# A mixture-of-experts layer: residual rows added by GpSimd's stores between expert tiles, and a last stage of one copy

## What is computed

```python
xn = _layernorm(x, axis=-1)
x = x + _L1_attn_ref(xn, ...) + _L1_ffn_ref(xn, ...)
return x

# _L1_attn_ref ends with        return resid + out
# _L1_ffn_ref, for each token, over its two chosen experts:
act = silu(gh) * xh                       # h = x @ w1[e] + b1[e], split in two
out_e = act @ w2[e] + b2[e]
return jnp.sum(sel * weights[..., None], axis=2)
```

## Time and profile before

| | us |
|---|---|
| median of 3 runs | 2629.0 (2627.3 to 2629.4) |
| the profiled execution | 2626.0 |
| its span, first to last instruction | 2624.3 |
| layer0, routing and mamba, up to | 1879 |
| experts | 1879.0 to 2586.7 |
| combine | 2586.7 to 2624.3 |

### The profile page before, as it was taken

The page is one execution under the profiler, slowest core; times in us unless marked ns, Lnnn a source line. Parts: engine busy times, 40 slices in busy tenths (PEclk is TensorE's granted clock), DMA queues, the critical chain, the costliest instruction groups (busy, mean ns, idle before and its releaser), DMA issues. The chain is left out here.

```text
span 2624.3 us, 34884 instructions
## 1 busy us (share of the span) xinstructions
PE 2141.1 (82%) x10642; PEld 1531.1 (58%) x10642; DVE 1947.4 (74%) x2684; ACT 1373.9 (52%) x2317; POOL 1343.0 (51%) x953
## 2 busy tenths in 40 slices
PE   2799999999936777878787878776499999999992
PEld 1578777778721222324232324233299999999992
DVE  6654456554540898989898989899588888888882
ACT  1332223323216766666666666653277767767760
POOL 1102222112204989898989898987213433333331
PEclk8899999999966999999999999999899999999996
DMA  8011011110021222222222222222356666666646
GB/s 258 16 41 40 0 40 40 40 40 20 20 72 40 81 78 88 85 91 78 101 76 96 83 96 76 93 84 83 127 213 233 220 214 216 227 229 228 216 151 204
DMA packets 117624, 290.90 MB, mean 111 GB/s; under 512 B 21076, under 2 KB 94180, under 8 KB 98740
## 3 DMA queue, kind: packets, MB, share of 16 engines
q1 hardware_dynamic: 103252, 271.38, 29.5%
q0 software_dynamic: 14304, 18.75, 3.5%
HBM read 239.24 MB, written 50.85 MB: 111 GB/s over the span
## 5 line engine op out<-in xcount | busy, mean ns | idle before, releaser
L1004 POOL TENSOR_TENSOR m_work<-m_ux,m_bb 128x1024 f32<-128x1024 f32 x256 | 598.6, 2356 | 21.4 <-DVE m_hh L1199 18.4
L1144 ACT ACTIVATE m_da<-m_dl,m_A 128x512 f32<-128x512 f32 x512 | 348.2, 685 | 288.5 <-DVE m_hh L1199 287.7
L1283 PE MATMUL m_y<-m_work,m_ident 128*128 128x512 f32 x1024 | 497.6, 609 | 1.5 <-DVE m_work L1205 1.5
L1199 DVE TENSOR_TENSOR_SCAN m_hh<-m_da,m_work 128x512 f32<-128x512 f32 x256 | 298.4, 1208 | 107.4 <-POOL m_work L1004 107.1
L1734 PE MATMUL e_h<-e_xTh,e_w1h 128*128 128x256 f32 x1248 | 353.8, 283 | 16.5 <-DVE e_xTl L1670 16.5
L1734 PE MATMUL e_h<-e_xTl,e_w1h 128*128 128x256 f32 x1248 | 349.9, 280 | 0.0
L1734 PE MATMUL e_h<-e_xTh,e_w1l 128*128 128x256 f32 x1248 | 349.8, 280 | 0.0
L1205 DVE TENSOR_TENSOR m_work<-m_hh,m_cb 128x1024 f32<-128x1024 f32 x256 | 312.7, 1222 | 30.7 <-PE m_cb L1264 7.8
L1199 DVE TENSOR_TENSOR_SCAN m_hh<-m_da,m_carry,m_work 128x512 f32<-128x512 f32 x256 | 313.9, 1268 | 26.2 <-POOL m_work L1004 26.2
L1283 PEld LDWEIGHTS m_y<-m_work,m_ident 128*128 128x128 f32 x1024 | 199.9, 195 | 157.1 <-issue 144.9
L280 POOL TENSOR_TENSOR small<-mv,eps_ln 128x4 f32<-128x4 f32 x17 | 3.4, 199 | 550.4 <-DVE mv L398 550.4
(11 more groups left out here) (259 smaller groups left out, 4763.4 us busy)
## 6 DMA issues: line engine op xcount, KB each, us to landing
e_w<-in_w SPq DMA_DIRECT2D x39, 2048.0 KB, 7.5
m_bb<-scratch_bT SPq DMA_DIRECT2D x64, 1024.0 KB, 4.7
e_w<-in_w SPq DMA_DIRECT2D x39, 1024.0 KB, 10.0
scratch_rec<-x1p SPq DMA_DIRECT2D x39, 260.0 KB, 8.0
e_xg<-scratch_rec SPq DMA_DIRECT2D x39, 260.0 KB, 2.7
e_b<-in_b SPq DMA_DIRECT2D x39, 128.0 KB, 3.0
xt<-in_x SPq DMA_DIRECT2D x9, 512.0 KB, 5.4
xres<-in_x SPq DMA_DIRECT2D x8, 512.0 KB, 4.8
```

What stands on the lines that cost most here:

```text
L1004: pool.tensor_tensor(bx[:, u % NB], ux[q % 2][:, cols], slot.to_broadcast([P, HALF, T]), ALU.mult).then_inc(s_bx, 1)
L1144: act.activation(da[d % NA][:], dl[q % 2][:, e], ACT.Exp, scale=A[:, at:at + 1]).then_inc(s_exp, 1)
L1199: dve.tensor_tensor_scan(hh[:, u % 2, i], da[d % NA][:], bx[:, u % NB, i], 0.0 if q % 2 == 0 else carry[:, n % NST, e:e + 1], ALU.mult, AL ...
L1283: last = mm(y[:, i], ident[:], hc[:, u % 4, i], start=False, stop=(n % NST == NST - 1))
```

## The change

`experts` gets two buffers `xrow` of 128 rows, a table `at_row` of row numbers (column j holds T + 128 j + partition, the rows of `mo` for block j of the tokens), and three kinds of semaphores. GpSimd loads blocks 0 and 1 of `x1p` ahead of its loop. In round t (1 to 32), between the wait for the sums of tile t - 2 and the four small operations, it waits for block t - 1 and issues one indirect store that adds it to `mo`. In `weigh(t)`, for t below 32, between the multiplication and the two result stores, it waits until block t has landed in `mo` and loads block t + 2 into the buffer that is free.

`combine` becomes one DMA from `mo` to the output; nothing is loaded to the core and VectorE has no work in it. The number of bytes that pass a DMA engine in this stage goes from 12.6 MB to 4.2 MB.

```diff
@@ experts
         yo = [sb(f"yo{i}", [P, NS, D]) for i in range(2)]
+        xrow = [sb(f"xrow{i}", [P, D]) for i in range(2)]
+        at_row = sb("at_row", [P, NJ], I32)
+        s_row, row_in, row_out = sem("at_row"), [sem(f"row_in{i}") for i in range(2)], [sem(f"row_out{i}") for i in range(2)]
...
+        def load_row(pool, j):
+            if j < NJ:
+                pool.dma_start(xrow[j % 2][:], dram["x1p"][j * P:(j + 1) * P, :]).then_inc(row_in[j % 2], 16)
+
         def weigh(pool, t):
...
             pool.wait_ge(s_yw, t + 1)
+            if t < NJ:
+                pool.wait_ge(row_out[t % 2], 16 * (t // 2 + 1))
+                load_row(pool, t + 2)
             if t >= 1:
                 pool.wait_ge(y_out[1 - i], 16 * NS * ((t - 1) // 2 + 1))
...
             identity(pool, ident, s_id)
+            pool.iota(at_row[:], pattern=[[P, NJ]], base=T, channel_multiplier=1).then_inc(s_row, 1)
+            pool.wait_ge(s_row, 1)
+            load_row(pool, 0)
+            load_row(pool, 1)
             pool.wait_ge(texb_in, 16)
...
                 if t >= 2:
                     pool.wait_ge(y_out[i], 16 * NS * (t // 2))
+                if 1 <= t <= NJ:
+                    j = t - 1
+                    pool.wait_ge(row_in[j % 2], 16 * (j // 2 + 1))
+                    pool.indirect_dma_start(dram["mo"][:, :], bass.IndirectOffsetOnAxis(ap=at_row[:, j:j + 1], axis=0),
+                                            xrow[j % 2][:], None, compute_op=ALU.add).then_inc(row_out[j % 2], 16)
                 pool.tensor_copy(place[i][:], xg[i][:, :, D].bitcast(I32)).then_inc(s_place, 1)
@@ combine
-            for c in range(NCH):
-                for tile, src in ((xa, dram["x1p"]), (mo, dram["mo"][T:, :])):
-                    sp.dma_start(tile[:, c * SUB:(c + 1) * SUB], src[c * T:(c + 1) * T, :].rearrange("(s p) d -> p s d", p=P)).then_inc(x_in[c], 16)
-            for c in range(NCH):
-                sp.wait_ge(s_add, c + 1)
-                sp.dma_start(out[c * T:(c + 1) * T, :].rearrange("(s p) d -> p s d", p=P), xa[:, c * SUB:(c + 1) * SUB]).then_inc(out_done, 16)
-            sp.wait_ge(out_done, 16 * NCH)
...
-                dve.tensor_tensor(xa[:, cs], xa[:, cs], mo[:, cs], ALU.add).then_inc(s_add, 1)
+            sp.dma_start(out.rearrange("(p n) d -> p (n d)", p=P),
+                         dram["mo"][T:, :].rearrange("(p n) d -> p (n d)", p=P)).then_inc(out_done, 16)
+            sp.wait_ge(out_done, 16)
```

More of the change, by code:

```diff
@@ L1 @@
+import math
 from contextlib import ExitStack
@@ L1766, in combine @@
     with ExitStack() as ctx:
[L1767 to L1776, removed]
+        out_done = ctx.enter_context(nc.semaphore("c_out_done"))
         block = ctx.enter_context(nc.Block())
```

## The result

The changed kernel takes 2664.9 us (median of 4 runs, 2663.2 to 2667.2) against 2628.2 us (4 runs, 2623.8 to 2629.4): a ratio of 1.0143, 95% interval 1.0126 to 1.0161. It is 37 us slower. The forecast was 2679 us, in a range of 2622 to 2717.

The account below looks back on a forecast made before the run. Expert tiles were taken as TensorE-bound, the last stage as DMA-bound; a lengthened GpSimd loop would set the pace. 2624.3 - 15.0 + 0.5 + 65 = 2675 us, 2679 as a median; range 2622 to 2717.

Parts of the forecast that it names:

- closed loop: Expert stage: weights, sums, small operations, rows, weights again take 16.89 us and set the pace once lengthened; chance 0.63.
- The room of 0.3 us: Expert stage: the loop's 16.89 us against a tile of 17.17 leave 0.3 us of room per tile.
- The adding store: On GpSimd ahead of the four small operations: 1.56 us plus 0.05 to the next instruction, 1.61 us in the loop.
- VectorE's share: GpSimd's later small operations run into VectorE's pair of operations: 0.6 us per round, within 0 to 1.8.
- The row load's part: Row load ahead of the result stores: its 0.13 MB on the busy DMA engines adds about 0.3 us to the loop.
- slack of 3.4 us: Rows land 3.4 us before TensorE turns them; once that is used up, TensorE waits once per tile.
- The new wait: GpSimd's wait for the adding store's landing, after the next multiplication and ahead of the load: costs nothing unless later.
- The last stage: One copy of 4.19 MB takes 22.6 us (12.3 to 27.1) instead of 37.6; the stage gains 15.0 us.
- A: Rival: GpSimd's idle time is real, TensorE doesn't wait, only the last stage counts: 2614.5 us; chance 0.21.
- B: Rival: sums land a fixed 6.8 us after the second store, TensorE waits 0.8 us per tile: 2639 us; chance 0.11.
- C: Rival: adding store lands after more than 6.8 us, GpSimd waits ahead of the load: 2719 us; chance 0.05.
- D: Rival: last copy runs at the memory's slow bound or worse, changing the sum by 4.5 us; counted in the ranges.

Follow-up runs that it names:

- e4: The kernel before plus a GpSimd table fill that nobody reads, at the adding store's place, with no added DMA bytes: 2649.8 us, ratio 1.0092.
- e1: The changed kernel with GpSimd's adding store issued behind the four small operations instead of ahead of them: 2631.0 us, ratio 1.0017.
- e3: The changed kernel with SP issuing the next weights right behind the rows, ahead of the two biases: 2633.1 us, ratio 1.0028.
- e7: The changed kernel without the loads of w2 from the third tile on, 2 MB of weights per tile instead of 3: 2624.5 us, ratio 0.9988.
- e5: The changed kernel with four place and share buffers, and the sums' wait and adding store behind the small operations: 2604.5 us, ratio 0.9911.
- e8: The changed kernel without the loads of residual rows after the first two, adding stores and their waits kept: 2660.9 us, ratio 1.0124.
- e2: The changed kernel without row loads and adding stores between tiles, only the last stage as one copy: 2605.9 us, ratio 0.9921.
- e6: The changed kernel with both the adding store behind the small operations and SP's weights ahead of the biases: 2606.5 us, ratio 0.9918.

## Why the prediction was right

**The bound and the loop: right.** The argument that GpSimd's idle time lies inside a closed loop (weights, sums, small operations, rows, weights) with hardly any room held. Time alone, put into the loop, costs 23 us (e4). Shortening any of three different terms (e1, e3, e7) brought 32 to 40 us back, and opening the loop (e5) all 60.

**The room of 0.3 us: a reading that does not stand.** The 16.89 us are one round. In the kernel before, SP's way from the rows to the next weights takes 3.77 us in one round and 4.04 in the next, and the weights are mostly issued 16.9 and 17.4 us apart in turn. Averaged over two rounds the terms add up to the tile of 17.17, as terms of anything that repeats do, so their sum can't show room. What gives way is inside the small operations. The sums land anywhere from 10.7 to 11.35 us into the tile, but VectorE's pair runs from 9.75 to 11.6, and the second small operation is over at 11.9 in 22 of 26 tiles and at 11.7 in the others. The four operations take 1.56 us on average and 1.01 in a late tile of the changed kernel in which no pair meets them:

```profile
2627.89 0.18 POOL L1556 COPY e_place<-e_xg 128x2 int32<-128x2 int32 x1 [2.35 <-DMA scratch_mo<-e_yo,e_place]
...
2628.70 0.20 POOL L1561 TENSOR_TENSOR e_share<-e_share,e_xg 128x2 f32<-128x2 f32 x1
```

The room is thus some 0.5 us (an estimate, 1.56 less 1.01), more or less by where VectorE's pairs lie. The prediction's 0.3 came near it by luck.

**The size: 60 us against 65.** The terms were not all right:
- The adding store was put at 1.61 us; it takes 1.83 in the tile shown, and the small operations begin before it is over. Store and small operations together went from 1.56 to 3.33 us, +1.77.
- VectorE's share was put at 0.6 us per round on top of before, a third of its bounds of 0 to 1.8. It was mis-sized. The shortest of the 26 rounds has 2.83 us for store and small operations, the mean 3.33, so VectorE holds them for some 0.5 us; but it held the small operations of before for as long. On top of before that is about nothing, and the store is the whole of the 1.77. The averages hide a spread: single tiles take from 18.0 to 20.8 us.
- The row load's part was put at 0.32 us; by e8 it is 0.13.
- The round was 19.2 us on average, not 19.4.
- TensorE's clock was at no place in the sum; the five places at 0.50 above are inside the 60 us.
- The upper end of the range, 2717, lacks the 4.7 us from span to median that its lower end has; it should be 2721.
- 31 rounds and the slack of 3.4 us used up once: TensorE's first stall is 0.4 us and the next three 1.7 to 1.8; the last affected round takes 20.2 us, and the next one is 17.16 again, as the prediction said.

**The new wait: right in the changed kernel.** The wait ahead of the load costs nothing there. That it is not harmless in general, e1 shows.

**The last stage: right in sign, mis-sized.** The step "I take 8.39 MB at 410 GB/s, both ends lie in the same memory" failed. The tile view of the copy in the changed kernel:

```profile
L1793 SPq DMA_DIRECT2D out<-scratch_mo x1: 607/607/607, 2650.2 to 2650.2; - x1
...
DMA to landing us min/median/max: 14.8/14.8/14.8
```

14.8 us, not 22.6: near the lower bound, 12.3, in which each byte counts once, and far from the 27.1 in which reads and writes both count. Less the prediction's fixed 2.05 us it is 329 GB/s, an estimate; the profile shows the copy's last packets before 2662, 3 us ahead of the landing, so the split between fixed time and transfer is open. The stage gains 22.3 us, not 15.0. This error of 7 us and that of 5 in the loop both make the forecast too slow; together they are most of the 14 us by which 2679 missed 2664.9. Of the rest, 0.8 us is the reference to the median, which is 2628.2 with one more run.

**The rivals.** A (idle time is real) is out by the measurement. B (the sums land a fixed time after their store) is out by the changed kernel itself, 11.1 us after the second store where it was 6.8, and by e7, where it is 8.8. It describes the kernels whose weights are well ahead of the stores (6.8 to 6.9 us in before, e2, e5 and e6) and fails once they are not. C needs the wait ahead of the load, which ends with the multiplication. D did not occur; the copy was faster, not slower.

**Queues and the copy's rate.** In the three microseconds from 2481 the stores' queue moves one packet and the weights' queue 76, on 16 engines. At 2486 it is 40 beside 42. The Trainium skill ("DMA: Bandwidth & Descriptors", section "Queues, rings and completion order") says that an engine empties a packet of one queue before it turns to the next. The 40 beside 42 fit such turns; the one beside 76 does not follow from them alone, and whether the stores had packets ready then, no run shows. The Trainium skill's 207 to 214 GB/s per direction ("DMA: Bandwidth & Descriptors", section "Latency and other measured facts") are for copies of 128 pieces of 16 KB between memory tensors, at a row pitch of 512 KB or at a padded one of 4 MB. Here 4.19 MB landed in 14.8 us, 283 GB/s with all fixed time in it, so its figure does not carry over to this copy, and the measurement decides.

## What to carry to other kernels

Idle time of an engine is free only if nobody's release stands behind it: before putting work into a gap, follow who is released by the instruction after the gap, whether that release starts a transfer, and whether that transfer delays what ends the gap. If it does, it is a loop. Its terms add up to the pace whether it has room or not, so look for the term that gives way, or put a known time in and see what comes out (here 0.95 us in and 0.70 out, where the profile showed 9.8 us of idle time per tile). The remedy was not less work but another place: first the operations that release others, then the wait for slow landings, with a buffer more to allow that order; and a final addition that only needs a copy afterwards is worth moving, once it is out of the loop (25 us here).

## What the runs showed of the hardware

- A copy from memory to memory in pieces of 64 KB landed after 14.8 to 15.2 us for 4.19 MB; issued on two queues it was no faster.
- With two adding stores of 128 rows of 1 KB, the rows are in place 4.0 us after the issue of the second with no other traffic, and 11.1 us after it on average (up to 12.8) where 3 MB of weights are issued about when they are. How the two queues share differs: 1 packet to 76 in 3 us from 2481 and 40 to 42 at 2486 in the changed kernel, 28 to 22 at 2334 in e7.
- GpSimd's issue of a plain load of 128 rows took 0.63 us, a copying indirect store 1.00, an adding one 1.56.
- Small operations of GpSimd of 0.2 to 0.3 us lasted up to 2.6 us while VectorE split weights (tensor operations of 1.23 and 0.69 us in a row).
- After stalls of TensorE of 3.2 to 3.8 us its granted clock was 0.50 for 3.4 us, four times of four in the changed kernel; after its stalls of up to 1.95 us it was so once in 27. In e8 it was so after stalls of 3.31, 1.95 and 1.83 us.
